# A cross-attention block in float32 parts: another order of work between the first two groups, more filler matmuls ahead of the first scores, and gates on GpSimd

## What is computed

```python
x = layer_norm(hidden_states, ln1_w, ln1_b)
q = x @ q_w + q_b;  k = ctx @ k_w + k_b;  v = ctx @ v_w + v_b       # 16 heads of 16
attn = softmax(where(mask, q @ k.T * 0.25, min))
hidden = (attn @ v) @ cproj_w + cproj_b + hidden_states
y = layer_norm(hidden, ln2_w, ln2_b)
y = gelu_tanh(y @ fc_w + fc_b) @ proj_w + proj_b
return hidden + y
```

## Time and profile before

| | us |
|---|---|
| median of 3 executions | 226.4 |
| lowest, highest | 226.09, 231.07 |
| the profiled execution, its own time | 227.06 |
| its span, first to last instruction | 225.3 |
| busy: TensorE, VectorE, ScalarE, GpSimd | 213.3, 176.7, 127.3, 90.1 |

### The profile page before, as it was taken

The page is one execution under the profiler, slowest core; times in us unless marked ns, Lnnn a source line. Parts: engine busy times, 40 slices in busy tenths (PEclk is TensorE's granted clock), DMA queues, the critical chain, the costliest instruction groups (busy, mean ns, idle before and its releaser), DMA issues.

```text
span 225.3 us, 7604 instructions
## 1 busy us (share of the span) xinstructions
PE 213.3 (95%) x3154; PEld 198.1 (88%) x3154; DVE 176.7 (78%) x376; ACT 127.3 (57%) x272; POOL 90.1 (40%) x104
## 2 busy tenths in 40 slices
PE   6898699998999999999999999999999999999995
PEld 6887688887989899999999998989999999899994
DVE  3698559967999797979798797979797679778461
ACT  3668148356824893369616971589248943673240
POOL 5356123339771384119510761248212811314200
PEclk9999589699999999999999999999999999999999
DMA  5989992105900195009700690039001920100101
GB/s 184 250 260 232 225 270 90 63 4 134 238 9 4 58 234 136 3 27 213 190 5 4 171 238 20 1 106 225 6 1 52 225 59 4 50 6 0 47 3 47
DMA packets 21940, 23.06 MB, mean 102 GB/s; under 512 B 1554, under 2 KB 20626, under 8 KB 21906
## 3 DMA queue, kind: packets, MB, share of 16 engines
q1 hardware_dynamic: 21008, 21.84, 40.2%
q10 hardware_dynamic: 898, 0.74, 1.1%
HBM read 7.62 MB, written 2.10 MB: 43 GB/s over the span
## 4 chain that ended last, share of the span: by engine, by line
PE 69%; DMA 9%; DVE 5%; POOL 5%; issue 5%; SPq 3%; ACT 2%; ACTq 0%; POOLq 0%
PE bank L1143 19%; PE bank L1144 15%; PE bank L1145 15%; DMA stack_kq<-parts 6%; PE scores L1173 4%; PE bank L1160 3%; PE bank L1239 3%; PE scores L1203 3%; PE bank L1246 3%; SPq L364 2%; DMA x_in<-in_x 2%; POOL rs L589 1%; DVE mx L876 1%; PE bank L1185 1%; DMA stack_kq<-n_t 1%
## 5 line engine op out<-in xcount | busy, mean ns | idle before, releaser
L1143 PE MATMUL bank<-proj_hi,g_hi 128*128 128x256 f32 x128 | 38.1, 298 | 0.2 <-DVE g_lo L944 0.2
L1143 PE MATMUL bank<-z_hi,fc_hi 128*128 128x256 f32 x128 | 37.6, 294 | 0.0
L1144 PE MATMUL bank<-z_hi,fc_lo 128*128 128x256 f32 x128 | 36.1, 282 | 0.0
L1144 PE MATMUL bank<-proj_hi,g_lo 128*128 128x256 f32 x128 | 36.0, 281 | 0.0
L1145 PE MATMUL bank<-z_lo,fc_hi 128*128 128x256 f32 x128 | 36.0, 281 | 0.0
L1145 PE MATMUL bank<-proj_lo,g_hi 128*128 128x256 f32 x128 | 36.0, 281 | 0.0
L589 POOL TENSOR_TENSOR rs<-ve,power 128x1 f32<-128x1 f32 x16 | 10.5, 654 | 51.3 <-DVE ve L901 51.3
L921 DVE RECIPROCAL recip<-bank 128x256 f32<-128x256 f32 x16 | 28.0, 1752 | 2.7 <-PE bank L1246 2.7
L663 ACT ACTIVATE fc_raw<-bank,fc_bias 128x256 f32<-128x256 f32 x64 | 26.5, 468 | 6.2 <-PE bank L1145 6.1
L876 DVE TENSOR_REDUCE mx<-scores 128x16 f32<-128x1024 f32 x16 | 19.5, 1221 | 10.8 <-PE scores L1173 10.7
L1143 PEld LDWEIGHTS bank<-proj_hi,g_hi 128*128 128x128 f32 x128 | 24.1, 188 | 1.8 <-DVE g_lo L944 1.0
(11 more groups left out here) (133 smaller groups left out, 571.6 us busy)
## 6 DMA issues: line engine op xcount, KB each, us to landing
stack_kq<-parts SPq DMA_DIRECT2D x48, 256.0 KB
x_in<-in_x SPq DMA_DIRECT2D x8, 256.0 KB, 5.9
ctx_in<-in_ctx_t SPq DMA_DIRECT2D x7, 256.0 KB, 6.0
out<-y SPq DMA_DIRECT2D x7, 256.0 KB, 2.1
fc_raw<-in_fc_w SPq DMA_DIRECT2D x1, 1024.0 KB, 11.0
proj_raw<-in_proj_w SPq DMA_DIRECT2D x1, 1024.0 KB, 10.8
ctx_in<-in_ctx_t ACTq DMA_DIRECT2D x1, 256.0 KB, 4.1
w_raw_q<-in_q_w SPq DMA_DIRECT2D x1, 256.0 KB, 4.7
```

The lines of the kernel that those rows point to most:

```text
L1143: mm(out_ap, a_hi, b_hi, start=first, stop=False, skip_group_check=True)
L1144: mm(out_ap, a_lo, b_hi, start=False, stop=False, skip_group_check=True)
```

## The change

- TensorE: 60 fillers in place of 12 before the first scores; in the first full step `shift_first` (selectors) for group 1's second row, and half of `fc_chunk(c, 0)` ahead of it; `turn_z2` of group 0 moves ahead of `turn_maxima(a, 1)` of group 1; the fillers 4 + 14 + 8 become 20 + 6.
- VectorE: `hidden(b, 1)`, `variance2(b, 1)` and both `normal2` of group 0 come before `maxima(a, 1)`.
- ScalarE: `keep_maxima(b, 0)` behind the high part of the cproj weights; `o_lead(b, 1)` ahead of `second_q`; `high_of_z2` at the head of the first full step; no `stack_maxima` for group 1's second row.
- GpSimd: the low part of the cproj weights after the first maxima instead of the second; `third_k` of group 2 waits for `n_split` 3, `third_q` of group 2 for `z2_made` 2.
- SyncE: group 2's stack waits for group 1's first maxima in the stack, no longer for the second; all later counts of `n_stacked[1]` are one less.

```diff
--- before.py
+++ after.py
@@ -404,7 +404,10 @@
 
             def full_step(a, b, c, ahead=True):
 
-                sp.wait_ge(n_stacked[1], b.count(16))
+                if b.c == 1:
+                    sp.wait_ge(n_stacked[0], 16)
+                else:
+                    sp.wait_ge(n_stacked[1], b.count(16, -16))
                 if c.c:
                     store(Group(0, c.c - 1))
                 sp.wait_ge(shifted, a.count(4, -4))
@@ -524,17 +527,18 @@
                 rest_of_ctx(Group(0, 2))
                 third_k(a)
                 third_q(a)
-                pool.wait_ge(n_split, 2)
+                pool.wait_ge(n_split, 1)
                 rest_of_w("c")
                 pool.wait_ge(bias_ready, 2)
                 x_and_bias(b)
                 rest_of_o(b, 0)
+                pool.wait_ge(n_split, 3)
                 third_k(Group(0, 2))
                 rest_of_o(b, 1)
                 row_scale(b, 0)
                 row_scale(b, 1)
+                pool.wait_ge(z2_made, 2)
                 third_q(Group(0, 2))
-                pool.wait_ge(z2_made, 2)
                 x_and_bias(a)
                 pool.wait_ge(w_high["proj"], 1)
                 rest_of_proj(0)
@@ -628,9 +632,11 @@
 
             def keep_maxima(g, p):
                 act.wait_ge(n_turned, g.count(2, p + 1))
-                wait(act, n_stacked[p], g.count(16, -16))
+                wait(act, n_stacked[p], g.count(16, -16 * (p + 1)))
                 if g.c == 1:
                     act.wait_ge(shifted, 2 * p + 2)
+                elif g.c == 2 and p == 1:
+                    act.wait_ge(shifted, 8)
                 sc.copy(n_t[p][:], n_turn_ps).then_inc(n_kept, 1)
 
             def stack_maxima(g, p):
@@ -772,9 +778,9 @@
                 second_q(a)
                 high_of_fc(0)
                 high_of_z(Group(0, 2))
-                keep_maxima(b, 0)
                 act.wait_ge(w_loaded["c"], 16)
                 high(w_hi["c"], w_raw["c"], w_high["c"])
+                keep_maxima(b, 0)
                 high_of_fc(1)
                 exp(b, 0)
                 keep_maxima(b, 1)
@@ -786,23 +792,26 @@
                 second_k(Group(0, 2))
                 keep_maxima(a, 0)
                 stack_maxima(a, 0)
+                o_lead(b, 1)
                 second_q(Group(0, 2))
-                o_lead(b, 1)
                 act.wait_ge(w_loaded["proj"], 16)
                 high(proj_hi, proj_raw, w_high["proj"])
 
             def full_step(a, b, c, ahead=True):
+                if first_full(c):
+                    high_of_z2(c)
                 fetch_table(ACT.Exp)
                 if not first_full(c):
                     lead_k(a)
                 keep_maxima(b, 1)
-                stack_maxima(b, 1)
+                if not first_full(c):
+                    stack_maxima(b, 1)
                 if not first_full(c):
                     lead_q(a)
                 exp(b, 0)
                 if not first_full(c):
                     second_k(a)
-                high_of_z2(c)
+                    high_of_z2(c)
                 if not first_full(c):
                     second_q(a)
                 exp(b, 1)
@@ -1064,16 +1073,17 @@
                 dve.wait_ge(bias_summed, 3)
                 ve.tensor_tensor(fc_bias[:], bank4[:, 1, 0:MB], col[:, COLS["fc_b"]:COLS["fc_b"] + MB],
                                  ALU.add).then_inc(bias_ready, 1)
-                maxima(a, 1)
                 hidden(b, 1)
                 variance2(b, 1)
+                normal2(b, 0)
+                normal2(b, 1)
+                maxima(a, 1)
 
             def full_step(a, b, c, ahead=True):
-                normal2(c, 0)
                 if not first_full(c):
+                    normal2(c, 0)
                     left_k(a)
-                normal2(c, 1)
-                if not first_full(c):
+                    normal2(c, 1)
                     left_q(a)
                 rest_of_z2(c)
                 if ahead:
@@ -1189,7 +1199,7 @@
             def shift(g, p):
 
                 q, k = q_stack[g.slot], k_stack[g.slot]
-                pe.wait_ge(n_stacked[p], g.count(16))
+                pe.wait_ge(n_stacked[p], g.count(16, -16 * p))
                 if p == 0:
                     pe.wait_ge(maxed, g.count(2, 2))
                 else:
@@ -1260,13 +1270,16 @@
                                       w_lo["c"][:, k, :], k == 0, k == KC - 1)
                 last.then_inc(projected, 1)
 
+            def fc_half(g, m, h):
+                cols_m = slice(P * (2 * m + h), P * (2 * m + h) + P)
+                for k in range(KC):
+                    last = three_pass(fc_bank(g, m)[:, h, :], fc_hi[:, k, cols_m], fc_lo[:, k, cols_m],
+                                      z2_hi[:, k, :], z2_lo[:, k, :], h == 0 and k == 0, k == KC - 1)
+                return last
+
             def fc_chunk(g, m):
-                bank = fc_bank(g, m)
                 for h in range(2):
-                    cols_m = slice(P * (2 * m + h), P * (2 * m + h) + P)
-                    for k in range(KC):
-                        last = three_pass(bank[:, h, :], fc_hi[:, k, cols_m], fc_lo[:, k, cols_m],
-                                          z2_hi[:, k, :], z2_lo[:, k, :], h == 0 and k == 0, k == KC - 1)
+                    last = fc_half(g, m, h)
                 last.then_inc(fc_made, 1)
 
             def make_k(a):
@@ -1375,7 +1388,7 @@
                 make_q(a)
                 make_v(a, 0)
                 make_v(a, 1)
-                keep_clock(scores[:, 0, 0:P], 12)
+                keep_clock(scores[:, 0, 0:P], 60)
                 pe.wait_ge(stacks_set[0], 16)
                 first_score(b)
                 turn_z(Group(0, 2))
@@ -1415,36 +1428,44 @@
                 sums_of_fc(range(MB // 2, MB)).then_inc(bias_summed, 1)
                 project(b, 1, a)
                 make_v(Group(0, 2), 1)
-                keep_clock(bank1[:, 0, 0:P], 4)
+                keep_clock(bank7[:, 0, 0, :], 20)
+                pe.wait_ge(k_left, 3)
+                turn_z2(b)
+                keep_clock(bank7[:, 0, 0, :], 6)
                 pe.wait_ge(bias_ready, 3)
                 turn_maxima(a, 1)
+
+            def first_chunks(b, c):
+
+                pe.wait_ge(z2_split, 1)
+                pe.wait_ge(w_split["fc"], KC)
+                pe.wait_ge(n_kept, 4)
+                fc_half(c, 0, 0)
+                shift_first(b, 1)
+                weigh(b, 0)
+                fc_half(c, 0, 1).then_inc(fc_made, 1)
+                pe.wait_ge(hid_made, 2)
+                fc_chunk(c, 1)
 
             def full_step(a, b, c, ahead=True):
                 if not first_full(c):
                     make_k(a)
                     turn_maxima(b, 1)
-                if not first_full(c):
                     make_q(a)
                 shift(b, 0)
-                if not first_full(c):
+                if first_full(c):
+                    first_chunks(b, c)
+                else:
                     make_v(a, 0)
-                else:
-                    keep_clock(bank7[:, 0, 0, :], 14)
-                pe.wait_ge(k_left, a.count(1, 1))
-                turn_z2(c)
-                if not first_full(c):
+                    pe.wait_ge(k_left, a.count(1, 1))
+                    turn_z2(c)
                     make_v(a, 1)
-                else:
-                    keep_clock(bank7[:, 0, 0, :], 8)
-                shift(b, 1)
-                weigh(b, 0)
-
-                pe.wait_ge(z2_split, c.count(1, 1))
-                if first_full(c):
-                    pe.wait_ge(w_split["fc"], KC)
-                fc_chunk(c, 0)
-                pe.wait_ge(hid_made, c.count(2, 2))
-                fc_chunk(c, 1)
+                    shift(b, 1)
+                    weigh(b, 0)
+                    pe.wait_ge(z2_split, c.count(1, 1))
+                    fc_chunk(c, 0)
+                    pe.wait_ge(hid_made, c.count(2, 2))
+                    fc_chunk(c, 1)
                 pe.wait_ge(gelued, c.count(4, 1))
                 fc_chunk(c, 2)
                 weigh(b, 1)
```

## The result

| us | before | after |
|---|---|---|
| median of 4 executions each, same chip | 226.25 | 230.75 |
| lowest, highest | 225.75, 231.07 | 229.2, 231.41 |
| ratio, 95% interval | | 1.0191 [1.0144, 1.0239] |
| profiled execution, its span, mean clock | 227.06, 225.3, 0.977 | 230.16, 228.4, 0.985 |

The change makes the kernel about 2% slower. The forecast was 225.8, and 230.75 lies outside the range of 223.8 to 227.9. One thing has to be known for all tables here: executions of one kernel spread over some 10 us (the kernel before: 222.9 to 233.4 over 117 executions on four chips), and the ratios compare the lower, undisturbed ones only, so that a ratio and the medians beside it can differ by 1%.

What follows compares the result with a forecast made beforehand. TensorE, busy 95%, was taken as the bound. With front gain 2.25 us, reorder and stall 1.1, TensorE gained about 0.9, ScalarE 0.55; the smaller, off the median 226.4, gave 225.8 us, range 223.8 to 227.9.

Steps and rivals of the forecast that it cites:

- The front, its start: Before the first scores: 60 fillers keep the clock at 2.4 GHz, so the maxima of (b, 1) start 2.25 us earlier.
- The cover of 0.3 us: Before the first scores: fillers end at 24.4 us, scores start at 24.66 whatever happens, leaving 0.3 us idle.
- The front, its way down: From the maxima of (b, 1) to the second `sums_of_fc`: no late DMA, so the 2.25 us gain carries through.
- F: Time won in the front by the fillers, 2.25 us, carried to the end of the second `sums_of_fc`.
- Clock at 41 us: Second low-clock stretch (0.50 at 41 us), after 1-column matmuls and short scores: expected to stay, its cost left in.
- the rival that takes it away: Low stretch at 41 us goes because its work moved: 1.2 us more gain, 224.6, or 223.5 without stall; chance 0.16.
- `normal2` and T: Group 0's second normalised row: `normal2` takes 0.40 us instead of 1.24, ending at T = 49.97, 1.65 us earlier.
- The stall of the small operation: Group 1's second maxima: the second small VectorE operation waits for GpSimd's `xb`, 1.1 us taken, bounds 0 and 2.3.
- The clock's fall in the new gap: Rival around `turn_z2`: clock falls in TensorE's new idle time, costing 1.7 us, time 227.6; chance 0.17.
- The hold at `o_lo`: Product on `o_lo`, 65.8 us: TensorE waits some 0.4 us there and is held to ScalarE's smaller gain, 0.55 us.
- The sum: Whole kernel: TensorE gains about 0.9 us, ScalarE 0.55; the smaller counts, giving 225.8 us from the median 226.4.
- the front gives nothing: Rival: the clock falls all the same or is already high unprofiled; 228.1 with the stall, 227.0 without; chance 0.10.

Runs made afterwards that it cites:

- f2: Kernel before with 60 fillers and the proj weights' load held until the first weigh is done: median 224.52 us, ratio 0.997.
- f4: Kernel after with proj load held, `xb` gated on `n_split` 4, and 5 more 512-column fillers in the gap before the last turned maxima: 226.13 us, ratio 1.0001.
- h2: Kernel before with 60 fillers and the proj load held, the same kernel as f2 on another chip: 224.2 us, ratio 0.9995.
- h4: Kernel after with proj load held and `xb` gated on `n_split` 4, the same kernel as f3 on another chip: 225.28 us, ratio 1.0044.
- f3: Kernel after with the proj load held until the first weigh is done and GpSimd's `xb` gated on `n_split` 4: 224.92 us, ratio 0.9937.
- g2: Kernel after with only GpSimd's `xb` gated on `n_split` 4, proj load early: 229.19 us, ratio 1.0139.
- e2: Kernel after with 12 fillers in place of 60 before the first scores: median 227.93 us, ratio 1.0047.
- e3: Kernel after with SyncE holding the proj load, and the loads behind it, until the first weigh is done: 226.67 us, ratio 1.0003.
- f1: Kernel after, unchanged, measured again on another chip against the kernel before: median 230.54 us, ratio 1.0247.
- g3: Kernel after with only 5 more 512-column fillers in the gap before the last turned maxima, proj load early: 229.73 us, ratio 1.0124.
- g4: Kernel after with proj load held, `xb` gated on `n_split` 4, and 12 fillers in place of 60: 224.56 us, ratio 0.9885.
- h3: Kernel after with proj load held, `xb` gated and 12 fillers, the same kernel as g4 on another chip: 226.13 us, ratio 1.0013.

## Why the prediction was wrong, point by point

- **The front, its start: right.** The clock stood at 1.00 from 20 us on and the maxima of (b, 1) began at 28.35 against 30.58, 2.23 earlier (2.25 predicted). The cover of 0.3 us was not there, though: the fillers began at 21.40 and not at 20.75, and the scores started right behind them, at 24.85.
- **The front, its way down: wrong, and this is the step that failed**: "Between them and 46.65 the chain is compute on TensorE, VectorE and ScalarE without a DMA that lands late, so I carry F = 2.25 us down". There is one DMA that no line of the kernel issues, by all signs TensorE's own instructions, and it lands late: TensorE stood 2.43 us in `weigh(b, 0)`. The forecast's F of 2.25 us was a loss of 0.33 by then: `fc_bias`, right behind the second `sums_of_fc`, began at 47.02 against 46.69, which is 2.58 us off. The trace of before held the hint, a stop of 0.27 without a releaser that ends at 35.28; it isn't among the idle times that the prediction went by the earlier trace rows.
- **Clock at 41 us**: left as a cost, and the rival that takes it away did not come. In all 18 profiles a low stretch begins between 36.0 and 41.1 us, with the stops and without them (f2, f4, h2, h4), so it is not the stops that make it.
- **`normal2` and T: right.** 0.41 for the second one, and z2 ended 3.29 us behind the start of `fc_bias`, where the sum had 3.28.
- **The stall of the small operation: right.** 1.12 beside `xb` (1.1 predicted), removed by the gate (0.17 in f3, g2 and h4). By the Trainium skill (SBUF — State Buffer, "SBUF: two separate sides") the port pair is locked for a whole instruction, and this trace agrees: L893 ended 0.03 us after `xb`. What I had not drawn from it is that the wait is in the change's own hand: one gate on `n_split` 4 removes it.
- **The clock's fall in the new gap** (chance 0.17): it happened in the profiled execution. The Gelu of chunk 0 was forecast for 55.65; with the 2.58 of the front it comes to 58.23, and it came at 59.30. The rest, 1.07 us, stands beside the slow half chunk and selectors (some 1.1 us over the sum) and is taken as the price of the fall, for which I had 1.7. It also fell in e2, after a gap of 1.49; not in e3 and f1, after 1.34 and 1.30.
- **The hold at `o_lo`: half right.** It is the place where the time passes to TensorE, with 0.17 us idle and not 0.4, as in before.
- **The sum.** Forecast -0.55, profile +3.12: 2.58 for the front and 1.07 for the clock make 3.65 of the 3.67 between them. The rival "the front gives nothing", with the stall, said 228.1, and with the fall added the kernel would be at 229.8: neither was priced together, and a front that gives less than nothing (-0.33) was in no case. The range was built of single mishaps, of which two came at once.

What stays open: that holding the load takes the loss back is shown by e3, against f1, g2 and g3, which keep it. That the stops are fetch waits is inferred: from the packet that comes 2.4 to 3.0 us before TensorE resumes in every such stop, from the fixed count of matmuls, and from the packets that come sooner with the load held; the profile has no line that says so. Holding the load leaves stops of 0.24 (e3), 1.09 (g4) and 1.28 us (h3), so something else in the queues delays the packet too. The gap before `turn_maxima(a, 1)` goes with the stall in after, but some 0.4 us of it remains in h3 with the stall away, and g3's profile can't tell what part of its loss is clock. In executions that aren't profiled, the split between stop and clock isn't known either, nor what the 1.4 us are by which the medians grew more than the profiled executions.

## What to carry to other kernels

Count instructions as a transfer too: before filling idle time with many small matmuls, look at the instruction queue in the DMA view, find where the blocks end and when each packet comes, and keep large loads that nobody needs yet from being issued in between. Read idle time put down to "issue" as a possible fetch wait even if it is 0.3 us: here such a stop of 0.27 us grew to 2.43 when TensorE came earlier, and took the whole gain. Measure a kernel again in another set before believing a gain under 1%. And where an edit lets one engine's operation start at the moment when another's short one comes, gate the long one behind it.

## What the runs showed of the hardware

- **Instruction blocks.** Packets of 0.02 MB on the instruction queue; TensorE resumes 2.4 to 3.0 us after the one that it is taken to lack. The packet for the 347th matmul (12 fillers) came at 32.6 and 32.8 us with the 1 MB load early and at 30.0 to 31.2 in four profiles with it held; the one for the 474th (60 fillers) at 34.3 to 34.8 in five and at 30.9 to 32.3 in six. The 13 stops took 0.2 to 3.27 us. The Trainium skill (Runtime: NRT & Kernel Launch, "Instruction fetch mechanics") has refills in blocks of 256 instructions, which agrees with 126 matmuls and their weight loads between two stops; it calls the cost of crossing a block's end mostly hidden, and here 2.43 us were not.
- **A small operation can be held until a large one ends.** VectorE's operation of 16 columns took 1.12 us beside a GpSimd operation of 1.27 us with two SBUF inputs (after, e2, e3), 0.17 alone.
- **Low clock with a busy TensorE.** It was granted 1.2 GHz from 37.4 to 57.8 us in g2 and 38.6 to 52.3 in f3, busy for 20.4 of the 20.4 us and 13.4 of the 13.7, while another execution of f3's very kernel (h4) has a mean clock of 0.992. Fillers before the stretch did not prevent it, and nothing in these runs says what ends it.
